# Attention over 8 sequences plus a 16-expert layer: projection jobs cut into 64-row halves and laid among the score matmuls, shift rows read by ScalarE, lo parts of the context made by GpSimd

## The reference, cut to what matters

```python
# x: (8, 1024, 256) float32; 16 heads of 16; scale folded into q
x = x + layernorm(attention(layernorm(x)))   # q, k, v and out projections 256x256 with biases
x = x + layernorm(experts(layernorm(x)))     # 16 experts of width 128, weights of the best 8, one shared expert

def attention(x):
    q, k, v = (split_heads(x @ w.T + b) for w, b in qkv)
    ctx = merge_heads(softmax(q @ k.T / 4) @ v)              # for every head
    return ctx @ out_w.T + out_b
```

## Time and profile before

| | |
|---|---|
| median of 3 runs | 2856.01 us (2855.09 to 2858.19) |
| the profiled execution | 2851.14 us, span 2849.4 us |
| mean granted TensorE clock | 0.989 |
| busy over the span: PE, DVE, ACT, POOL | 96%, 78%, 57%, 34% |
| one middle batch, from `pv` of unit 0 to the next batch's | 194.66 us |

### The profile page before, as it was taken

The page is one execution under the profiler, slowest core; times in us unless marked ns, Lnnn a source line. Parts: engine busy times, 40 slices in busy tenths (PEclk is TensorE's granted clock), DMA queues, the critical chain, the costliest instruction groups (busy, mean ns, idle before and its releaser), DMA issues.

```text
span 2849.4 us, 47584 instructions
## 1 busy us (share of the span) xinstructions
PE 2746.2 (96%) x16514; PEld 1685.8 (59%) x16514; DVE 2233.9 (78%) x4679; ACT 1632.6 (57%) x3095; POOL 954.7 (34%) x997
## 2 busy tenths in 40 slices
PE   5999999999999999999999999999999999999997
PEld 3434333343343343333433388888888888888886
DVE  4898998999999999999999667666666666666654
ACT  1477777777777777777778843333333333333332
POOL 4041462543533624625435545111111111111112
PEclk8899999999999999999999999999999999999999
DMA  5313422343234134333432323222222222232221
GB/s 88 55 27 57 65 60 54 57 85 57 56 63 64 42 65 64 64 56 59 69 64 72 88 78 105 82 79 77 73 82 83 79 79 71 83 82 79 79 74 54
DMA packets 136639, 197.32 MB, mean 69 GB/s; under 512 B 22336, under 2 KB 84816, under 8 KB 134352
## 3 DMA queue, kind: packets, MB, share of 16 engines
q1 hardware_dynamic: 136400, 194.29, 30.6%
HBM read 108.74 MB, written 17.30 MB: 44 GB/s over the span
## 4 chain that ended last, share of the span: by engine, by line
PE 82%; SPq 6%; DVE 5%; ACT 4%; issue 2%; POOL 1%; DMA 1%; POOLq 0%; ACTq 0%; DVEq 0%
PE o_bank L557 14%; PE y_bank L680 13%; PE g_bank L666 13%; PE u_bank L666 13%; PE sm_bank L547 12%; PE st_bank L535 7%; PE job_bank L581 4%; SPq L339 3%; DVE score_max L1036 3%; ACT probs L925 3%; PE job_bank L590 2%; PE job_bank L602 1%; SPq L352 1%; SPq L363 1%; SPq L364 1%
## 5 line engine op out<-in xcount | busy, mean ns | idle before, releaser
L1036 DVE TENSOR_REDUCE score_max<-sm_bank 128x1 f32<-128x512 f32 x2048 | 1302.3, 681 | 114.4 <-PE sm_bank L547 110.7
L925 ACT ACTIVATE probs<-st_bank 128x512 f32<-128x512 f32 x2023 | 1077.8, 601 | 319.0 <-PE st_bank L535 316.5
L547 PE MATMUL sm_bank<-qk_stack 64*128 64x512 f32 x2048 | 804.3, 465 | 18.7 <-DMA qk_stack<-qk_stack 10.5
L535 PE MATMUL st_bank<-qk_stack 64*128 64x512 f32 x2023 | 753.3, 453 | 30.1 <-ACT probs L925 24.5
L547 PEld LDWEIGHTS sm_bank<-qk_stack 64*128 64x128 f32 x2048 | 332.5, 187 | 581.6 <-DVE score_max L1036 537.9
L557 PE MATMUL o_bank<-probs,v_quad 128*32 128x512 f32 x4096 | 545.5, 605 | 9.1 <-ACT o_sb L833 7.0
L1193 DVE TENSOR_TENSOR h<-gate_act,u_bank 128x512 f32<-128x512 f32 x256 | 176.2, 688 | 312.9 <-ACT gate_act L887 312.9
L887 ACT ACTIVATE gate_act<-g_bank 128x512 f32<-128x512 f32 x272 | 162.4, 597 | 418.1 <-PE u_bank L666 418.0
L535 PEld LDWEIGHTS st_bank<-qk_stack 64*128 64x128 f32 x2023 | 313.7, 184 | 99.6 <-ACT probs L925 74.6
L898 ACT ACTIVATE h_hi<-h 128x512 fp32r<-128x512 f32 x272 | 172.2, 633 | 325.5 <-DVE h L1196 287.8
L680 PE MATMUL y_bank<-f_w_hi,h_hi 128*128 128x256 f32 x1088 | 311.7, 286 | 0.1
(11 more groups left out here) (200 smaller groups left out, 3874.5 us busy)
## 6 DMA issues: line engine op xcount, KB each, us to landing
cb<-comb_dram SPq DMA_DIRECT2D x256, 256.0 KB, 3.6
qk_stack<-qk_parts SPq DMA_DIRECT2D x360, 128.0 KB
x_in<-in_x SPq DMA_DIRECT2D x8, 1024.0 KB, 6.6
o_part<-o_sb SPq DMA_DIRECT2D x256, 32.0 KB, 2.0
sum_part<-o_sb SPq DMA_DIRECT2D x256, 32.0 KB, 2.0
x_res<-in_x SPq DMA_DIRECT2D x16, 512.0 KB, 3.9
x<-x_res SPq DMA_DIRECT2D x16, 512.0 KB, 3.1
f_x_in<-x SPq DMA_DIRECT2D x16, 512.0 KB, 3.9
```

What stands on the lines that cost most here:

```text
L535: mm(bank_of(tile)[:, :], k_stack[q][p][rows, kc * CH:(kc + 1) * CH], q_stack[q][p][rows, f * HALF:(f + 1) * HALF], start=True, stop=True) ...
L547: mm(sm_bank[n % RING][:, :], q_stack[q][p][rows, tok:tok + CH], k_stack[q][p][rows, half * HALF:(half + 1) * HALF], start=True, stop=True ...
L925: nc.scalar.activation(probs[kc % 2][:, j, :], bank_of(4 * U + j)[:, :], ACT.Exp).then_inc(exp_done, 1)
L1036: v.reduce_max(score_max[f][:, HC * (2 * p + e) + c, half:half + 1], sm_bank[n % RING][:, :], AX_X).then_inc(smax_read, 1)
```

## The change

- QK, V, OP and XT jobs are cut into two row halves, e = 0 and e = 1, each into three thirds. A third is one matmul (QK) or two (V, OP) with a contraction of 64. They are laid between the score and maximum tiles so that neighbours are on different row halves. `job_rows_done`, a new semaphore, makes the e = 1 half wait until the e = 0 half has finished in the same bank, and the second part wait for the first. SH stays a 128-row transpose.
- The order in a unit starts with `pv`; then follow the score tiles 4U+6 to 4U+9, in all batches: the special order of the last batch from unit 50 is gone. The order of heads (`HEAD_AT`) and of maximum tiles (`MAX_AT`) alternates the row halves.
- The jobs' units move: the fourth QK job from units 37 and 38 to 39 and 40, the V jobs from 39 to 48 to 42 to 51, the last four QK jobs from 51 to 60 to 52 to 62.
- ACT writes the shift row. POOL makes the lo part of the context, with two instructions in place of one of DVE, and a new semaphore between them. The last batch's two late splits stay on DVE.

```diff
-JOBS = {
-    23: ("XT", 1, 0, None), 24: ("XT", 1, 1, None), 27: ("XT", 1, 2, None), 28: ("XT", 1, 3, None),
-}
-for _s in range(STEPS):
-    JOBS[8 * _s + 1] = ("SH", 0, _s + 1, None)
+JOBS = {}
+for _i, _u in enumerate((1, 9, 17, 25, 32, 41, 49, 57)):
+    JOBS[_u] = ("SH", 0, _i + 1, None)
+for _i, _u in enumerate((22, 24, 26, 28)):
+    JOBS[_u] = ("XT", 1, _i, None)
...
-        ("OP", -1, 0, (5, 6, 7, 8)), ("OP", -1, 2, (15, 16, 20, 21)),
-        ("QK", 1, 0, (29, 30, 31, 32, 35, 36, 37, 38)), ("V", 1, 0, (39, 40, 43, 44, 45, 46, 47, 48)),
-        ("QK", 1, 4, (51, 52, 53, 54, 55, 56, 59, 60))):
+        ("OP", -1, 0, (5, 7)), ("OP", -1, 2, (15, 20)), ("QK", 1, 0, (30, 33, 36, 39)),
+        ("V", 1, 0, (42, 44, 47, 50)), ("QK", 1, 4, (52, 55, 58, 61))):
     for _n, _u in enumerate(_at):
-        JOBS[_u] = (_kind, _off, _i + _n // 2, _n % 2)
+        for _part in range(2):
+            JOBS[_u + _part] = (_kind, _off, _i + _n, _part)
...
+                if third == 0:
+                    if e == 1 or part == 1:
+                        pe.wait_ge(job_rows_done, rows_done[0])
...
+                elif kind == "QK":
+                    m, half, n = i // 4, i // 2 % 2, "qk"[i % 2]
+                    a, w = PARTS[third]
+                    last = mm(job_bank[:, :], w_parts[n][w][rows, part, m * 128:(m + 1) * 128],
+                              xT[a][rows, part, half * HALF:(half + 1) * HALF],
+                              start=(part == 0 and third == 0 and e == 0), stop=(part == 1 and third == 2 and e == 1))
...
-                    scores(0)
-                    scores(1)
-                    if late:
-                        scores(2)
-                        scores(3)
-                    maximum(0, 0)
                     if last and u == UNITS - 1:
                         gu(0, 0, 0, True)
                     pv(U, S, s, kc)
...
+                        job_rows(JOBS[u], b, 0, 0)
+                        st(4 * U + 6)
+                        job_rows(JOBS[u], b, 0, 1)
+                        maximum(0)
+                        job_rows(JOBS[u], b, 0, 2)
+                        st(4 * U + 7)
+                        maximum(1)
+                        maximum(2)
+                        st(4 * U + 8)
+                        job_rows(JOBS[u], b, 1, 0)
+                        maximum(3)
+                        job_rows(JOBS[u], b, 1, 1)
+                        st(4 * U + 9)
+                        job_rows(JOBS[u], b, 1, 2)
+                    else:
+                        st(4 * U + 6)
+                        maximum(0)
+                        st(4 * U + 7)
+                        maximum(1)
+                        maximum(2)
+                        st(4 * U + 8)
+                        if u in JOBS and not skipped(JOBS[u], first, last):
+                            job("SH", b, JOBS[u][2])
+                        maximum(3)
+                        st(4 * U + 9)
...
+            def split_lo(B, f, k):
+                wait_apart(pool, ctx_hi, split_no(B, f, k) + 1, passed["pool"])
+                g.tensor_scalar(o_part[f][:, :], o_part[f][:, :], bias[:, 2, k:k + 1], None, ALU.add).then_inc(ctx_biased, 1)
+                wait_apart(pool, ctx_biased, split_no(B, f, k) + 1, passed["pool"])
+                g.tensor_tensor(cT[f][1][:, k, :], o_part[f][:, :], cT[f][0][:, k, :].bitcast(F32),
+                                ALU.subtract).then_inc(ctx_split, 1)
```

More of the change, by code:

```diff
@@ L67, in skipped, with among_scores @@
     return off == -1 and first or off == 1 and last or last and kind == "SH" and i == STEPS
+def among_scores(u, first, last):
+    return u in JOBS and JOBS[u][0] != "SH" and not skipped(JOBS[u], first, last)
 def wait_apart(engine, semaphore, value, passed):
@@ L552, in pv @@
                 q = s // 2
-                if kc == 0 and not (isinstance(S, int) and S == 0):
+                if kc == 0 and S > 0:
                     pe.wait_ge(o_stored, S)
@@ L706, in _ @@
             before.pop(0)
-            for j in range(RING):
-                st(0, 0, 0, j, 0)
+            for tile in range(6):
+                st(tile)
             def batch(b, first, last):
@@ L824, in _ @@
                 job(kind, 0, i, first_bank[n % 2])
+            job("SH", 0, 0)
             for i in range(4):
```

129 lines of the change are left out of this document (78 added, 51 removed).

## The result

The change makes the kernel slower: 2938.45 us (median of 4 runs, 2933.84 to 2940.33) beside 2857.1 us before, ratio 1.0284 with a 95% interval of 1.0271 to 1.0297. The profiled execution of after took 2940.33 us (span 2938.5), 89.2 us more than that of before. The expert half is unchanged: the last `pv` lies at 1731.80 us instead of 1642.54, and that is 89.3 us.

A forecast was written before the change was run, and what follows sets the result against it. Bound: the PE–ACT loop in units without a job, PE in job units, the SP queue around loads. Interior batches −5, first 0, last −1, tail +7 make +1 on 2851.14 us; forecast 2856 us, no change, range 2815 to 2895.

The forecast's parts named there:

- What bounds the kernel: Units without a job: a loop through ACT, 2.70 us; job units: PE, 3.23 us; shift rows: SP queue, margin 1.5 us.
- The pair pace of the job units: Job units: 64-row pairs on two row halves cost 0.34 us for the first, then 0.23 each.
- the first rival: Job units: halves do not keep the pair pace, 3.36 us a unit; 2921 us in all; chance 0.22.
- So 2.91 in place of 3.22: A job unit: 2.81 us from pair slots plus 0.1 for the job_rows_done wait; 3.19 still at a step's end.
- units 15 to 40: Interior batch: job units at 2.91 us and others at 2.80 bring 79.7 us to 75.4, a change of −4.3.
- The read of a job at its new place: ACT's read begins about 0.13 us behind pv; 0.64 us of slack takes nearly all, 0.1 added per unit behind a job.
- so this is hidden: POOL's two operations per split, 10 us a batch, cost nothing since gather runs a step later; otherwise up to 2.6 us each.
- the named sign that POOL's splits hold up the SP queue: Listed as a sign of being wrong: POOL's splits appear as a releaser of the SP queue.
- Units 41 to 46: +5.5: Seven batches: a later stack load delays step 6's shift rows, PE waits in unit 46, the stretch is 5.5 us longer.
- Units 47 to 63: −2.1: Interior batch: 3 units at 3.19, 10 at 2.91 and 4 at 2.80 us make 49.9 instead of 52.0.
- Units 0 to 14: Interior batch: change 0, since PE waits for step 2's shift rows, which land 43.9 us in whatever PE does.
- The tail: Last batch, units 50 to 61: pv waits on the 2.70 us loop, 34.1 us instead of 26.89, so +7.

The follow-up runs named there:

- e2: The changed kernel with the last maximum tile and the last score tile of a job unit exchanged on PE: 2914.1 us, ratio 1.0216 to before.
- e3: The changed kernel with the lo parts of the context back on DVE and off POOL: 2933.5 us, ratio 1.0271 to before.
- e10: The changed kernel with step 6's shift rows before the stack load, last maximum tile later, old tail order, lo parts still on POOL: 2874.4 us, ratio 1.0080.
- e1: The changed kernel with step 4's gather and step 6's shift rows ahead of the first stack load in the SP queue: 2894.0 us, ratio 1.0130.
- e5: The changed kernel with the last batch's score tiles from unit 50 on around pv as before the change: 2933.5 us, ratio 1.0280.
- e12: The changed kernel with shift rows of steps 6 and 2 queued earlier, last maximum tile later, lo parts on DVE, old tail order: 2843.5 us, ratio 0.9960.

## Why the prediction was wrong, point by point

- **What bounds the kernel:** right in kind. The loop of 2.70 us for a unit without a job, PE for a job unit, and the SP queue's order behind the load are what the runs moved.
- **The pair pace of the job units:** right, 0.23 us where the first rival had 0.34. The wait on `job_rows_done` costs nothing. The sentence of the Trainium skill weighed there ("TensorE: Matmul & The Clock Gate", Part 3, The mechanism) does not hold as it stands in these traces either: pairs with loads for both row halves in flight start 0.23 apart in every unit looked at. The same section also names a load into a background weight buffer; whether that is at work here no run shows.
- **"So 2.91 in place of 3.22":** the step that failed first. The sum counted pair slots and left out the ring of three maximum banks: with the first and the fourth maximum tile 1.18 us apart by DVE's reduction, a job unit is 3.17 to 3.20. It missed 0.27 us for each of the 19 job units that it counted in units 15 to 40 and 47 to 63, and 0.38 for the four XT units of a batch, which it had put at 2.80. e2 showed it: with one tile moved the unit is 2.94.
- **The read of a job at its new place:** right (about 0.14 us behind `pv`, most units behind it 2.83), except for unit 60 at 3.15, over the 2.9 named as a sign of being wrong; there the fourth maximum tile waits 0.37 us for DVE. What stays hidden in the change shows when PE gets faster: 3.0 in e2.
- **POOL's two operations, "so this is hidden":** wrong by a mechanism that the prediction did not have. Small DVE operations beside them take 1.25 instead of 0.16 us. In the change this makes unit 41 last 4.39 us instead of 3.29 (e3) and accounts for 1.1 us of the stack load's delay; the other 0.5 is there with lo parts on DVE too. The gather does not wait for them in the middle batches of the change, only because it stands behind the late stack load; with the queue's order mended it waits 4.2 to 4.5 us, the named sign that POOL's splits hold up the SP queue. In the change most of the loss drowns in the wait (e3: 5 us, not clear of noise); in the mended kernel it costs 25 us (e10).
- **"Units 41 to 46: +5.5":** the mechanism was right (wait in unit 46, shift rows as its releaser, seven times), the size was not: +8.1, since the load began 3.33 us behind `pv` of unit 41 and not 1.7, and `pv` of unit 47 came 1.03 and not 0.66 behind the tile.
- **The clock:** missing altogether. Behind the wait unit 47 takes 4.55 to 5.16 us, while in e1 it takes 3.4 to 3.6 in six of seven batches, all at full clock.
- **"Units 47 to 63: −2.1":** wrong by 5.2 us: 1.7 for the clock in unit 47 (4.9 as a mean, forecast 3.19), 10 × 0.27 for the maximum ring, 0.33 for the step's end in unit 63 (3.52, forecast 3.19) and 0.35 for unit 60 (3.15, forecast 2.80), which make 5.1.
- **Units 0 to 14:** right, −0.6. DVE's relief shows in units 4 and 12, behind the splits: 2.74 instead of 3.06 us.
- **The tail:** +7.7 for +7, the size in part by luck. The loop gave 2.67 us a unit for the 2.70 named, but unit 50 took 3.83, at a clock of 0.57, and unit 54 was shorter than forecast (3.55 for 3.9). The trace of e5 confirms the cause (28.79 us), its time does not show a gain.

The misses for an interior batch, times seven, are about 30 us in units 15 to 40 (4.3 each), 18 in units 41 to 46 (2.6) and 36 in units 47 to 63 (5.2), less 4 in units 0 to 14: 80 of the 88 us between the 2852 forecast for the profiled execution and its 2940.3. The other 8 lie in the last batch, which got 14.4 us longer for the forecast 6: its units 15, 42 and 48 to 50 ran in part at the lower clock. The largest wait was forecast; what turned "no change" into 2.8% is that the gain that was to pay for it never came, and that the wait itself was dearer.

## What to carry to other kernels

When matmuls are packed closer, count not only the slots but each ring: how long from a tile to the one that takes its bank, the consumer's time included. An engine's queue of transfers is a schedule too: moving a job by two units moved every transfer behind it, and the cheapest mend was two lines in that queue's order (44 us), once for each load checked who needs it next. Price an edit where no wait covers it, and look at the waits again when you do: beside the wait, undoing the halves or POOL's lo parts changed little (7 and 5 us by the medians, not clear of noise); with the wait and the ring mended, the halves gain 22 us and POOL's lo parts cost 25, most of that through transfers that wait for them.

## What the runs showed of the hardware

**DVE beside POOL.** A DVE operation on 128x4 elements, from and to on-chip memory, took 1.25 or 1.29 us instead of 0.16 when POOL was in an operation on 128x512, and ended within 0.03 us of it; the maxima, which read the matmul banks, kept their 0.68 us throughout (0.62 in a row). The Trainium skill ("SBUF — State Buffer", Who interferes with whom) says that a `tensor_scalar` of DVE in its mode with two ports and an operation of POOL exclude each other for a whole instruction, the one issued later waiting, while `tensor_reduce` never contends. The traces agree for these two, with these durations: the operations above are `tensor_scalar`, and no reduction is lengthened. But a small `tensor_tensor` is caught too, `row_max`, which usually takes 0.17 us. It could be read before the change, in the first trace (second batch, timeline of all engines):

```profile
318.93 1.28 POOL L1442 TENSOR_TENSOR recip<-recip,recip_tmp 128x512 f32<-128x512 f32 x1
319.02 1.22 DVE L1043 TENSOR_TENSOR row_max<-score_max 128x16 f32<-128x16 f32 x1
```

It too ends 0.03 us behind POOL's; the same section says that a DVE instruction with two inputs in the on-chip memory contends with one of POOL that reads it.

**The clock falls behind short stalls.** The seven waits of 3.54 to 5.77 us in unit 46 of after were each followed by a stretch at 1.2 GHz (granted clock of unit 47 0.50 to 0.72); of the shorter stalls in unit 41 some were: unit 42 ran partly at the lower clock in three of the six middle batches of after, behind a unit 41 of 4.38 to 4.68 us, and at full clock in the other three, behind one of 4.38 or 4.39. It strikes the tail as well. The same unit 50 of the last batch, in the same written order, in e5 and in e12:

```profile
1691.96:1694.86 2.90, 2.90 (x17) 1.16 (x16) 0.00 (x0) 1.89 (x5) 0.00 (x0) 1.00 0.15 38
```

```profile
1596.73:1601.93 5.20, 5.20 (x17) 1.91 (x16) 0.41 (x1) 1.88 (x5) 0.00 (x0) 0.50 0.39 114
```

The tail of e12 took 35.29 us in this execution and that of e5 28.79. Why the clock falls in the one and not in the other stays open.
